# One mirrored block in three turned by VectorE and two DMA passes instead of by TensorE

## What is computed

```python
h = jnp.maximum(_layernorm(x, axis=-1), 0.0)
norm2 = jnp.linalg.norm(h, axis=1, keepdims=True)
cos = beta[0] * (h @ h.T) / (norm2 @ norm2.T + 1e-07)
P = jax.nn.softmax(cos + (1.0 - adj) * -1000000000.0, axis=1)
x = x + P @ h
h = jnp.maximum(_layernorm(x, axis=-1), 0.0)
deg = jnp.clip(jnp.sum(adj, axis=1, keepdims=True), 1.0)
x = x + h @ W_self + (adj @ h / deg) @ W_neigh
```

## Time and profile before

| | |
|---|---|
| median of 3 runs | 492.41 us (492.33 to 492.5) |
| the profiled execution, whole | 492.51 us |
| its span (first to last instruction) | 490.7 us |
| PE / DVE / ACT / POOL busy | 95% / 56% / 59% / 52% of the span |
| granted TensorE clock | 0.999 of full speed |
| loop over pairs / second part | about 30 to 349 us / 349 to 491 us |

### The profile page before, as it was taken

How to read it: one execution, slowest core, us unless ns; L and a number is a source line. 1 busy time by engine, 2 the same in 40 slices (tenths; PEclk the granted TensorE clock), 3 DMA queues, 4 the chain that set the end, 5 groups by cost and what they waited for, 6 DMA issues and landing times.

```text
span 490.7 us, 12317 instructions
## 1 busy us (share of the span) xinstructions
PE 466.7 (95%) x5200; PEld 390.5 (80%) x5200; DVE 276.6 (56%) x672; ACT 288.5 (59%) x437; POOL 255.8 (52%) x249
## 2 busy tenths in 40 slices
PE   0879999999999999999999999998998999999997
PEld 1747888888788887888878887886787888888886
DVE  6966656667565685656856675775766410122232
ACT  2999788776977768976598669777864000000000
POOL 3889777666866658765587478666662000000000
PEclk9999999999999999999999999999999999999999
DMA  8167865765787555976569647846500000000000
GB/s 248 23 74 157 160 144 114 121 150 75 135 167 144 118 80 106 185 153 116 72 126 173 117 65 137 164 68 97 74 7 1 17 7 23 23 23 23 24 23 21
DMA packets 31547, 46.05 MB, mean 94 GB/s; under 512 B 2560, under 2 KB 24320, under 8 KB 31488
## 3 DMA queue, kind: packets, MB, share of 16 engines
q0 software_dynamic: 10368, 9.44, 25.5%
q1 hardware_dynamic: 21120, 35.79, 23.2%
HBM read 71.43 MB, written 2.10 MB: 150 GB/s over the span
## 4 chain that ended last, share of the span: by engine, by line
PE 86%; DVE 5%; ACT 4%; POOL 2%; issue 1%; DMA 1%; SPq 0%; DVEq 0%; POOLq 0%; ACTq 0%
PE ps L1114 22%; PE ps L991 17%; PE ps L1002 10%; PE ps L1097 6%; PE ps L1094 6%; PE ps L1096 6%; PE ps L1069 5%; PE ps L1072 5%; PE ps L1071 5%; ACT word L566 1%; ACT ps L567 1%; DVE adj_t L655 1%; DMA x_sb<-in_x_dram 1%; POOL adj_t L398 1%; PE ps L1026 1%
## 5 line engine op out<-in xcount | busy, mean ns | idle before, releaser
L421 POOL TENSOR_TENSOR near<-word,adj_t 128x1024 f32<-128x1024 f32 x72 | 144.9, 2013 | 101.7 <-DVE word L800 98.2
L566 ACT ACTIVATE word<-ps,small 128x512 f16<-128x512 f32 x144 | 136.1, 945 | 74.3 <-PE ps L991 74.2
L800 DVE TENSOR_TENSOR word<-ps,word 128x512 f16<-128x512 f32 x144 | 106.0, 736 | 95.7 <-ACT ps L567 95.6
L1114 PE MATMUL ps<-table,adj_t 128*128 128x257 f16 x1024 | 114.7, 274 | 0.0
L991 PE MATMUL ps<-unit_t 128*128 128x512 f16 x432 | 107.2, 379 | 3.8 <-DVE word L800 2.0
L1114 PEld LDWEIGHTS ps<-table,adj_t 128*128 128x128 fp8e4 x1024 | 100.0, 98 | 13.5
L567 ACT ACTIVATE ps<-ps,small 128x512 f32<-128x512 f32 x144 | 108.0, 750 | 0.0
L1094 PE MATMUL ps<-table,near 128*128 128x129 f16 x576 | 102.6, 219 | 1.6 <-POOL near L421 1.5
L1097 PE MATMUL ps<-table,near 128*128 128x129 f16 x576 | 102.9, 222 | 0.0
L1096 PE MATMUL ps<-table,near 128*128 128x128 f16 x576 | 102.6, 219 | 0.0
L1069 PE MATMUL ps<-table,far 128*128 128x129 f16 x448 | 79.9, 219 | 0.5 <-DVE far L810 0.3
(11 more groups left out here) (86 smaller groups left out, 440.8 us busy)
## 6 DMA issues: line engine op xcount, KB each, us to landing
stage<-in_adj_dram SPq DMA_DIRECT2D x56, 512.0 KB, 4.6
adj_t<-in_adj_dram POOLq DMA_DIRECT2D x72, 128.0 KB, 4.0
x_sb<-in_x_dram SPq DMA_DIRECT2D x4, 512.0 KB, 6.3
x_again<-in_x_dram SPq DMA_DIRECT2D x7, 256.0 KB, 5.6
out_dram<-x_sb SPq DMA_DIRECT2D x7, 256.0 KB, 2.8
far<-in_x_dram SPq DMA_DIRECT2D x1, 256.0 KB, 5.0
out_dram<-x_sb SPq DMA_DIRECT2D x1, 192.0 KB, 2.0
adj_t<-in_L_gnn_W_neigh_dram SPq DMA_DIRECT2D x1, 64.0 KB, 5.7
```

The source lines that it names most:

```text
L421: pool.tensor_tensor(ring(near, k), ring(word, k), adj_t[:, near_adj(k)], ALU.mult).then_inc(s_near, 1)
L566: act.activation(half(word16, k, c, 0, HIGH, TPS), score(k, c), ACT.Exp, bias=exp_bias, scale=exp_scale)
L800: dve.tensor_tensor(half(word16, k, c, 0, LOW, TPS), score(k, c), half(word16, k, c, 0, HIGH, TPS), ALU.subtract).then_inc(s_elo, 1)
L1114: return pe.matmul(ps[:, agg_bank(g, t), 0:TW], adj_t[:, at:at + P], tab(b), start=(b == 0), stop=(b == T - 1))
```

## The change

For 17 of the 56 far pairs, every third from pair 8 on through strip 4, the transpose leaves PE. `moved_pairs` names them: 8, 11, 14, 17, 21, 24, 27, 30, 33, 36, 39, 42, 45, 48, 51, 55, 58. For a moved pair k:

- DVE, `transpose_blocks(k)`: one instruction transposes `word` (128x1024 fp32) in 32x32 blocks into the new buffer `packed32`. It stands in iteration k-1, where `mask_far(k)` stood.
- SP, `store_blocks(k)`, in its step k+3: waits for the transpose, stores `packed32` (512 KB) to the device-memory tensor `bounce`.
- SP, `fetch_blocks(k)`, in its step k+4: waits for the store, fetches the four groups of 32 partitions with four DMAs of 128 KB into the new buffer `slot`. The blocks are now in their final partitions.
- DVE, `mask_moved(k)`: `slot` times the mirrored adjacency tile, into `far`.
- PE, `attend_far(k)`: three pairs later, in the iteration of its host (17 goes to 20, 51 to 54, 58 to 62, which have no far side of their own). The host is mostly itself a moved pair, whose own far side goes three further on.

`far` slots, spills and semaphore counts follow the new order of attending (`ORDER`). ACT's wait before `exps(k+2)` is for `s_blocks` (the DVE transpose) in place of `s_turn`.

```diff
+                if k - 3 in MOVED:
+                    store_blocks(k - 3)
+                if k - 4 in MOVED:
+                    fetch_blocks(k - 4)
...
-                    if PAIR[k - 2][2]:
-                        act.wait_ge(s_turn, FAR_BEFORE[k - 1])
+                    if k - 2 in MOVED:
+                        act.wait_ge(s_blocks, M_BEFORE[k - 1])
+                    elif PAIR[k - 2][2]:
+                        act.wait_ge(s_turn, N_BEFORE[k - 1])
...
+            def store_blocks(k):
+
+                sp.wait_ge(s_blocks, M_BEFORE[k] + 1)
+                sp.dma_start(bounce.rearrange("a p x -> p a x"), packed32[:, :].rearrange("p (a x) -> p a x", a=4)).then_inc(s_stored, 16)
+
+            def fetch_blocks(k):
+
+                sp.wait_ge(s_stored, 16 * (M_BEFORE[k] + 1))
+                for a in range(4):
+                    sp.dma_start(slot[32 * a:32 * a + 32, :].rearrange("s (q x) -> s q x", q=4), bounce[a].rearrange("(q s) x -> s q x", q=4)
+                                 ).then_inc(s_moved, 16)
...
+            def transpose_blocks(k):
+
+                dve.wait_ge(s_elo, 2 * k + 2)
+                if M_BEFORE[k] >= 1:
+                    dve.wait_ge(s_stored, 16 * M_BEFORE[k])
+                dve.transpose(packed32[:, :].rearrange("p (a ct r) -> p a ct r", a=4, r=32),
+                              ring(word, k).rearrange("p (ct a r) -> p a ct r", a=4, r=32)).then_inc(s_blocks, 1)
+
+            def mask_moved(k):
+
+                m, i = FAR_BEFORE[k], M_BEFORE[k]
+                dve.wait_ge(s_moved, 64 * (i + 1))
...
+                dve.tensor_tensor(
+                    ring(far, at).rearrange("p (c t q r) -> p c t q r", c=2, t=TPS, q=4),
+                    slot[:, :].rearrange("p (q c t r) -> p c t q r", q=4, c=2, t=TPS),
+                    far_adj(k, adj_t).rearrange("p t (c q r) -> p c t q r", c=2, q=4), ALU.mult).then_inc(s_far_m, 1)
...
-                    if PAIR[k][2]:
-                        spill(k)
-                    if k + 1 < NP and PAIR[k + 1][2]:
+                    if FAR_AT[k] is not None:
+                        spill(FAR_AT[k])
+                    if k + 1 in NORMAL:
                         mask_far(k + 1)
+                    if k + 1 in GUEST:
+                        mask_moved(GUEST[k + 1])
+                    if k + 1 in MOVED:
+                        transpose_blocks(k + 1)
```

More of the change, by code:

```diff
@@ L22, in gnn_program @@
     FAR_BEFORE = [sum(m < k for m in FAR) for k in range(NP + 1)]
+    MOVED, HOST = moved_pairs(PAIR)
+    NORMAL = [k for k in FAR if k not in MOVED]
+    N_BEFORE = [sum(m < k for m in NORMAL) for k in range(NP + 1)]
+    M_BEFORE = [sum(m < k for m in MOVED) for k in range(NP + 1)]
+    GUEST = {HOST[k]: k for k in MOVED}
+    FAR_AT = [GUEST.get(k, k if k in NORMAL else None) for k in range(NP)]
+    ORDER = [k for k in FAR_AT if k is not None]
     FIRST = [min(k for k in range(NP) if PAIR[k][0] == s) for s in range(NS)] + [NP]
@@ L77, in gnn_program @@
         far = sb("far", [P, 2 * TILE], fp32)
+        packed32 = sb("packed32", [P, TILE], fp32)
+        slot = sb("moved_words", [P, TILE], fp32)
         x_again = sb("x_again", [P, ROWS], fp32)
@@ L822, in spill @@
                 else:
-                    if k == FIRST[s]:
-                        dve.wait_ge(s_spill, FAR_BEFORE[k])
+                    same = [j for j in FAR if PAIR[j][0] == s - 1 and PAIR[j][1] == p][0]
+                    if same in MOVED or ORDER.index(k) == min(ORDER.index(j) for j in FAR if PAIR[j][0] == s):
+                        dve.wait_ge(s_spill, ORDER.index(k))
                     dve.tensor_tensor(rows, two_rows(FAR_ACC), rows, ALU.add).then_inc(s_spill, 1)
@@ L995, in turn @@
             def turn(k, c, t):
-                m = FAR_BEFORE[k]
-                if c == 0 and t == 0 and m >= 1:
-                    pe.wait_ge(s_far, m)
+                n = N_BEFORE[k]
+                if c == 0 and t == 0 and n >= 1:
+                    pe.wait_ge(s_far, n)
                 if t == 0:
@@ L1060, in attend_far @@
                 s, p, _ = PAIR[k]
-                m = FAR_BEFORE[k]
-                pe.wait_ge(s_far, m + 1)
-                if m >= 1:
-                    pe.wait_ge(s_spill, m)
+                at, n = ORDER.index(k), N_BEFORE[k]
+                if k in MOVED:
+                    pe.wait_ge(s_far_m, M_BEFORE[k] + 1)
+                else:
+                    pe.wait_ge(s_far, n + 1)
+                if at >= 1:
+                    pe.wait_ge(s_spill, at)
                 for c in range(2):
@@ L1067, in attend_far @@
                         rows = s * TPS + t
-                        high, low = half(far16, m, c, t, HIGH), half(far16, m, c, t, LOW)
+                        high, low = half(far16, at, c, t, HIGH), half(far16, at, c, t, LOW)
                         pe.matmul(far_acc(c), high, tab(rows, D, TW), start=c == 0 and t == 0, stop=False,
@@ L1219, in pair_order, with moved_pairs @@
     return order, steps, pairs
+def moved_pairs(order):
+    far = [both for _, _, both in order]
+    moved, host = [], {}
+    k = 8
+    while k < len(order) and order[k][0] < 5:
+        if not far[k]:
+            k += 1
+            continue
+        at = k + 3
+        moved.append(k)
+        if order[at][0] >= 5:
+            at = min(i for i in range(at, len(order)) if not far[i])
+        host[k] = at
+        k = at
+    return moved, host
 def packed(adj):
```

42 lines of the change are left out of this document (27 added, 15 removed).

## The result

The changed kernel takes 501.29 us (median of 5 runs, 500.09 to 506.82) against 492.36 us for the kernel before beside it: ratio 1.020, 95% interval 1.018 to 1.023. Forecast were 482.5 us, with 477.2 to 491.5 for 8 in 10. It is slower by 8.9 us where 10.0 us of gain were forecast: 18.8 us more than the sum.

The account below looks back on a forecast made before the run. TensorE, 95% busy, was taken to bound the kernel: 492.5 less 15.0 for its transposes, plus 2.1, 1.8 and 1.0 lost again, gives 482.4, stated as 482.5 us; range for 8 in 10: 477.2 to 491.5.

Parts of the forecast that it names:

- TensorE's gain: On TensorE, 17 moved pairs lose their transposes at 0.88 us each: 15.0 us less.
- The VectorE transpose: On VectorE, the new transpose of 1024 columns was taken as 1.22 us, between bounds of 0.70 and 2.01.
- Rival 2: A slow VectorE transpose of 2.01 us eats every group's slack: 9.0 us on top, 491.4 us; chance 0.13.
- Does the place hold?: Mask and transpose in VectorE's iteration, laid out for one group: all waits hold by 0.6 to 0.8 us, TensorE stays last.
- cover: ScalarE's 1.96 us idle ahead of its next exponentials: nothing gained from it, it absorbs the wait for the transpose.
- (a): The new mask's two SBUF operands meet GpSimd's conversion in 7 of 17 pairs, 0.3 us lost each: 2.1 us.
- (b): Groups holding a pair without far side: shorter iterations make TensorE wait for VectorE, 6 x 0.3 = 1.8 us lost.
- (c): Pair 8 without guest, 0.2 us, and pairs 55 and 56 both without far products, 0.8: together 1.0 us lost.
- The way over device memory: Store and fetches stay hidden: round trip 10.2 us, range 7.2 to 15.0, words there just before the mask needs them.
- Rival 3, the ring: Transpose, store, fetch and mask limit the loop once the round trip exceeds 12.0 us: 496 to 508 us; chance 0.17.
- DMA traffic rises by 1 MB per group, 75 GB/s on 129: Added store and fetch traffic in the loop, set against 248 GB/s moved in the first 12 us; no time charged.
- converted more than 5 us later: Tile loads k+4 and k+5 on SyncE's queue go about 1 us late, but their conversions come over 5 us later.

Follow-up runs that it names:

- e1: The changed kernel without store and fetches, the new mask reading `packed32` as it is (wrong words, same other work): 496.80 us.
- e5: e3 without the way over device memory, so the transpose is at the front of VectorE's iteration and the mask reads `packed32`: 485.54 us.
- e6: e1 with the moved pairs' mask reading PSUM banks in place of `packed32`, transpose still behind the mask: 489.55 us.
- e7: e5 with the moved pairs' mask reading PSUM banks in place of an SBUF buffer: 482.12 us.
- e2: e1 plus transfers of the changed kernel's sizes at the same SyncE steps, with no engine waiting for their data: 500.27 us.
- e4: The changed kernel with store and fetches each one step later on SyncE's queue, so tile loads go first: 517.87 us.
- e10: e3 with one load, the `x_again` of strip 1, in SyncE's step 26 in place of 24: 488.45 us.
- e3: The changed kernel, whole, with the VectorE transpose moved to the front of VectorE's iteration and store and fetch waits added: 489.08 us.

## Why the prediction was wrong

**TensorE's gain: right.** 136 instructions gone, 0.88 us for eight of them in the chain; the first moved pair shows it undisturbed (from -0.1 to -1.0 by pair 11).

**The VectorE transpose: right.** 1.22 us taken, 1.239 measured in 17 cases. The estimate of 1.24 that the text drew from the Trainium skill ("VectorE: DVE Perf Modes", section "The three transpose paths") fits. Rival 2 is out.

**"Does the place hold?": the step that failed.** It laid out the group 21 to 24 and found 0.6 to 0.8 us of slack on all three counts. Moving the transpose alone gives 11.3 us (e1 to e5), 7.4 of it with a mask of 1.21 us throughout. Three things were wrong with the time line. It modelled one quiet group and took it for all 17: in the loop also stand the preparation of the tables and of the second layer, which take turns in the ring of score banks (1.47 us in iteration 10), and `new_rows` at the strip changes. It called ScalarE's 1.96 us of idle time "cover" to be used up: ScalarE then waits 12.1 us for the transpose, and its exponentials are what the next `low_part` and the next scores follow from, so a late group has little to recover with. And with 0.6 us left on each path it charged nothing for the place itself. How the 7.4 us divide between these the runs do not show.

**(a), the mask beside GpSimd: right mechanism, wrong size.** 2.1 us forecast, 7.2 measured (e1 to e6). The text had about 7 masks near 2.1 us. In `after` four of 17 were long (1.48, 2.04, 1.93 and 1.95 us, in the first four places), in e1 seven, 1.49 to 2.42. The count was right for e1, the price was not: 0.3 us each, "against 0.6 to 0.8 of slack" that wasn't there. In e1 the 17 masks are 5.5 us longer than in e6 (1536 against 1215 ns), and the kernel 7.2: all of it went through, and more. In `after` itself the masks are only 2.6 us longer than e6's; after the first four, none began while a GpSimd pass was running. So the 7.2 are a price in e1's order and not a share of `after` that could be read off its trace. With the transpose in front, 3.2 us of longer masks (1402 against 1211 ns) cost 3.4.

**(b) and (c), light groups and ends: not separated.** 2.8 us forecast; what is left in e7 is 4.8, and it holds these.

**The way over device memory: in time, but not free.** That the words arrive in time was right: VectorE waited 3.0 us for them in all, 1.0 at most, with 4.0 and 4.4 us for the legs at the median. Rival 3, the ring, is not what makes the median of `after`, although the measured time lies in the range given for it: e2 has no ring and takes 500.27. It is close, though. In the profiled execution the two legs are 13% of the chain that ended last, and e4 shows that the ring decides once the store goes one step later. "DMA traffic rises by 1 MB per group, 75 GB/s on 129" was somewhat high (180 in place of 129), and was priced at nothing: it costs 3.5 us without any wait for words (e2 against e1). And that the tile loads, about 1 us late, are "converted more than 5 us later" was the wrong sentence: their landing rose from 4.6 to 5.5 us at the median and from 7.0 to 10.6 at most, and the converters waited 34.4 us for tiles. SyncE also waited 116.4 us for transposes and 49.1 for stores with loads behind them. Much of that is time it would have waited anyway: before, it waited 301.4 us for converters to free a tile's slot, after only 104.5.

```profile
SPq L364 <- DVE packed L853: 116.4, 17, 13.2
SPq L370 <- DMA turned_blocks<-packed: 49.1, 17, 4.2
```

`x_again` between store and load was missed altogether.

**The sum again, with what was measured:** 492.4 - 10.2 (e7: transposes off, what light groups and ends cost in it) + 7.4 (place) + 7.2 (operand, in that place) = 496.8, plus 3.5 (traffic) and 1.0 (waits) = 501.3. These are steps between neighbouring kernels and depend on their order: the operand costs 3.4 where the place is good, and with the place good the way over memory costs 3.5 in all. Against the forecast the terms are 7.4 for a place priced at nothing, 5.1 too little for the mask (7.2 against 2.1), 2.0 too little for (b) and (c) (4.8 against 2.8) and 4.5 for a way over memory priced at nothing.

**Would it be worth making?** With the transpose in front the whole change gives 489.08 us, 0.8% faster than before (interval 0.5% to 1.1%), e10 (488.45) the same within the spread. These two are the best whole versions found.

## What to carry to other kernels

Taking work off the fullest engine pays in full only if what replaces it fits in a gap that is *idle in every iteration*; model the worst iteration (other work in the same ring, a strip's end), not the quietest, and put the new instruction where its engine already waits for something else. Idle time of an engine ahead of the next step of the chain is the loop's only reserve: an instruction that others wait for must not use it up. And 1 MB more for each group must be priced even where nobody waits for it: it lengthens the loads beside it. A mask that reads two SBUF operands has to be laid out against GpSimd's passes, one by one.

## What the runs showed of the hardware

- After two gaps of 2.42 and 2.65 us, TensorE's granted clock fell from full speed (2.4 GHz) to about half, its lower level of 1.2 GHz. The next eight transposes took 1.60 us of the chain in place of 0.88. The chain there, and the windows around it (same columns as above):

```profile
154.90 1.60 PE ps L1065 x8
```

```profile
143.00:149.00 6.00, 3.16 (x36) 1.94 (x33) 1.95 (x3) 3.89 (x5) 0.80 (x2) 1.00 0.95 207
149.00:153.00 4.00, 1.77 (x13) 1.74 (x14) 2.82 (x4) 2.45 (x4) 2.67 (x2) 0.55 0.44 142
153.00:157.00 4.00, 4.00 (x38) 3.99 (x37) 0.89 (x2) 1.97 (x3) 0.92 (x2) 0.59 0.94 193
```

Here the late tile loads are thus paid twice: once as idle time, once in slower products behind it. The clock over the profiled span was 1.00 in e1 and 0.986 in `after`.

- A 32-partition transfer from SBUF to SBUF takes SyncE 0.59 us to issue (median of 272), a 128-partition load 0.33.
- The spread of a kernel's four to six runs was larger where the kernel waited for transfers: 482.08 to 482.15 us for e7 and 489.48 to 489.64 for e6, but 484.06 to 486.93 for e5, 485.72 to 490.88 for e3 and 500.09 to 506.82 for `after`. e5 has no added transfer and differs from e7 in the mask's operand and the waits that go with it, so the meeting of VectorE and GpSimd may make a spread too; e1, with the same operands, has one of 0.7 us (496.45 to 497.16).
